# Two moves in a four-layer network kernel: the split of the last ffn's weights, and who mixes the second conditioning's weights

## The chip, the cores and the metric

The kernel runs on one core of a Trainium2 chip. The metric is the device time of one execution in microseconds, as a median over runs. The engines are named as in the profile: PE (TensorE matmuls, PEld their weight loads), DVE (VectorE), ACT (ScalarE), POOL (GpSimd) and SP (SyncE, which issues the transfers).

## The reference, cut to what matters

The input x is 16 blocks of 128 tokens with 128 features, float32. Four layers each add an attention of a conditioned x and an ffn of a conditioned x. Two places matter here.

The second conditioning of layer 0 mixes eight weight matrices for each block, with eight factors, under one mask. The attention of layer 3 has 16 heads of width 8, is causal, and stands just ahead of the last conditioning and the last ffn:

```python
# layer 0, second conditioning: y is the (16, 8) cond_8, weight (8, O, T), mask (O, T)
W[b] = sum_g y[b, g] * weight[g] * mask          # one 128x128 matrix for each block b
x2[b] = x[b] @ W[b].T + bias

# layer 3
score = einsum('bnqd,bnkd->bnqk', Q, K) / sqrt(8), masked causally; attn = softmax(score)
out = einsum('bnqk,bnkd->bnqd', attn, V) @ W_o.T
# last ffn, on a conditioned x
h = silu((x @ w1.T) * s1) * ((x @ w2.T) * s2)
h = gelu((h @ h1.T) * sh1); h = gelu((h @ h2.T) * sh2); return (h @ w3.T) * s3
```

## The kernel before, in words

x stays on the chip for the whole kernel. The 16 blocks are worked on in four chunks of four blocks. One ordered list of steps (`order`) is built first. Each engine's program then walks the whole list and issues its own part of each step, with semaphore waits between engines. So the order of steps is the order of every engine's queue, and there is no planner.

Much of the list is written by `in_order`. It takes items that have several stages, starts one new item per round, and in each round emits the new item's first stage and then the next stage of every item that is still live, youngest first. An attention is a list of 32 such items called heads (chunk n, block or head group j, half 0 or 1), plus projection items. In the last attention (`mh_attn(3, ...)`) the stages of one head are, in five or six successive rounds:

- scores on PE (lines 1677 to 1693; the mask is added by line 1686, the products by line 1693), and for every second head the masked copy of the keys, `kb`, on POOL (line 2796);
- row maxima on DVE (line 2318, two of them), a subtraction on DVE (line 2321), then the exponentials on ACT (lines 2024 and 2028);
- transposes on PE (`turn4`, lines 1607 and 1608) and their eviction by ACT (line 2033);
- the product with V on PE (line 1734), and for the second half the division on DVE (lines 2327 and 2329);
- for the last head of a chunk the output projection on PE (line 1741) and its addition on DVE (line 2332).

Halves 0 are "early": they read only 64 keys per block, so their row maxima, exponentials and transposes are half as large. A head takes two of four PSUM banks (`RA`) for its scores. The first bank is given back by the subtraction on DVE, the second by the exponentials on ACT that read it. The transposes use two other banks (`RB`), and the projections of the next chunk (lines 1659 to 1667) use banks of both rings.

**The split of the last ffn's weights.** The last ffn multiplies float32 numbers as two float32r parts each: a rounded part and the rest. `split_steps` makes eleven steps `wsplit`, one for each 512 of 5632 columns. In a step ACT copies 512 columns of BW to R1 in the rounded type (line 2173), and DVE subtracts the rounded part from the original (line 2743), waiting for ACT. Step number s is put behind the first stage of item 6 + 2s of the last attention's item list, so items 6, 8, ... 26 carry one each. In ACT's queue it stands ahead of that round's exponentials, in DVE's queue ahead of that round's row maxima. The result is first read by the last ffn (`l3_up`), after the attention and a conditioning.

**The mixed weights of the second conditioning.** During the first attention, `wbot_steps` puts one step `wbot` beside each of the 32 heads: four blocks b to b+3 at a time, eight factors g. In a step DVE does block b alone (line 2341 for g = 0, otherwise the multiply-add at line 2344, which the profile books under its helper, line 2211), and POOL does blocks b+1 to b+3: a product of 384 columns into a small buffer (line 2806) and an addition of it (line 2810). The buffers (`RWB`) are two, of 384 columns. POOL's queue holds these steps between the `kb` copies that the scores need. The step `cond2` on PE (line 1755), whose first one comes while the last heads of the attention are finishing, waits for the last `wbot` of DVE and of POOL.

Of the kernel before, what the change touches and what calls it, by code (L numbers as in the profile page):

```python
# [6 lines left out]
ALU = mybir.AluOpType  # L7
# [136 lines left out]
def build(nc, xT, cst, l0b, w8, b2, fw, fd, l1c, moe1, l1f, moe2, moe3, l2f, moe4, l3f, xs, ys, out):  # L144
    with ExitStack() as ctx:
# [448 lines left out]
        WBOT = A1[:, 8192:10240].rearrange("p (b o) -> p b o", b=16)  # L594
        RWB = Ring([A1[:, 10240 + 384 * k:10624 + 384 * k] for k in range(2)])
        WUG = BW[:, 6144:6912].rearrange("p (n o) -> p n o", o=128)
        WDN = BW[:, 6912:7296].rearrange("p (n o) -> p n o", o=128)

        def wbot_steps():
            def masked():  # L600
                sig["wmask"] = tick("wmask")
                step("wmask")
            steps = [masked]
            for b in range(0, NB, 4):
                for g in range(8):
                    def go(b=b, g=g):
                        at = step("wbot", b=b, g=g, mask=sig["wmask"], prev=sig.get(("wb", b)), prev_pool=sig.get(("wb3", b)),
                                  tmp=RWB.take() if g else None)
                        at["t"] = sig["wb", b] = sig["wbot"] = tick("wbot_dve")
                        at["part"] = sig["wb3", b] = sig["wbot_pool"] = tick("wbot_pool")  # L610
                        if g:
                            at["acc"] = sig["wb3", b] = sig["wbot_pool"] = tick("wbot_pool")
                            RWB.give(at["tmp"], at["acc"])
                    steps.append(go)
            return steps
# [36 lines left out]
        for n in range(NC):  # L652
            def c2(n=n):
                at = step("cond2", n=n, x=sig["x0", n], wbot=sig["wbot"], wbot_pool=sig["wbot_pool"], pa=RA.take(),
                          yfree=sig["Yfree", n])
                at["mm"] = sig["wbot_over"] = tick("c2_mm")
                at["y"] = sig["y0b", n] = tick("c2_y")
                RA.give(at["pa"], at["y"])
            items.append(([("x0", n)], [c2], ("y0b", n)))
# [777 lines left out]
        def split_steps():  # L1437
            steps = []
            for k in range(0, LO, 512):
                def go(k=k):  # L1440
                    at = step("wsplit", k=k, over=sig["moe4_over"])
                    at["hi"] = tick("l3_act")
                    at["t"] = sig["l3w"] = tick("l3_vec")
                steps.append(go)
            return steps
# [108 lines left out]
        for k in range(6, 6 + 2 * len(splits), 2):  # L1554
            f0, go = at3[k][1][0], splits[(k - 6) // 2]
            at3[k] = (at3[k][0], [lambda f0=f0, go=go: (f0(), go())] + at3[k][1][1:], at3[k][2])
        seq = (items + flat(seq[12:]) + flat(mix(m3, f2, m4, shared_items())) + at3 + cond_items("y3b", 3, "x3")
# [39 lines left out]
        def _(e):  # L1597
# [27 lines left out]
            for kind, at in order:  # L1625
# [122 lines left out]
                elif kind == "cond2":  # L1748
                    over(at["pa"])
                    w.wait_ge(*at["wbot"])  # L1750
                    w.wait_ge(*at["wbot_pool"])
                    w.wait_ge(*at["x"])
# [231 lines left out]
        def _(e):  # L1984
# [7 lines left out]
            for kind, at in order:  # L1992
# [171 lines left out]
                elif kind == "s2_up":  # L2164
                    for k in range(2):
                        over(at["r"][k])
                        w.wait_ge(*at["mm"][2 * k])
                        e.activation(at["r"][k].ap, at["pg"][k].ap, ACT.Silu).then_inc(at["silu"][k][0], 1)
                elif kind == "wsplit":
                    k = at["k"]  # L2170
# [28 lines left out]
        def _(e):  # L2199
# [17 lines left out]
            for kind, at in order:  # L2217
# [115 lines left out]
                elif kind == "wmask":  # L2333
                    w.wait_ge(*loaded["w8"])
                    e.tensor_tensor(W8, W8, bc_mid(c("maskT"), 8), ALU.mult).then_inc(sig["wmask"][0], 1)
                elif kind == "wbot":
                    b, g = at["b"], at["g"]
                    y = COND[:, 8 * b + g:8 * b + g + 1]
                    w.wait_ge(*at["mask"])
                    if g == 0:  # L2340
                        e.tensor_scalar(WBOT[:, b, :], W8[:, g, :], y, None, ALU.mult).then_inc(at["t"][0], 1)
                    else:
                        w.wait_ge(*at["prev"])
                        stt(WBOT[:, b, :], W8[:, g, :], y, WBOT[:, b, :], ALU.mult, ALU.add).then_inc(at["t"][0], 1)
                elif kind == "fq":
# [391 lines left out]
                elif kind == "s2_down":  # L2737
                    w.wait_ge(*at["mm"])
                    e.tensor_tensor(ch(X, at["n"]), v4(at["pb"].ap), ch(X, at["n"]), ALU.add).then_inc(at["t"][0], 1)
                elif kind == "wsplit":  # L2740
                    k = at["k"]
# [29 lines left out]
        def _(e):  # L2771
# [6 lines left out]
            for kind, at in order:  # L2778
# [19 lines left out]
                elif kind == "wbot":  # L2798
                    b, g = at["b"], at["g"]
                    to = WBOT[:, b + 1:b + 4, :]  # L2800
                    yb = COND.rearrange("p (b g) -> p b g", g=8)[:, b + 1:b + 4, g]
                    part = at["tmp"].ap.rearrange("p (b o) -> p b o", b=3) if g else to
                    w.wait_ge(*at["mask"])
                    if g:
                        over(at["tmp"])
                    e.tensor_tensor(part, bc_mid(W8[:, g, :], 3), bc_last(yb, 128), ALU.mult).then_inc(at["part"][0], 1)
                    if g:
                        w.wait_ge(*at["part"])
                        w.wait_ge(*at["prev_pool"])
                        e.tensor_tensor(to, to, part, ALU.add).then_inc(at["acc"][0], 1)  # L2810
# [148 lines left out]
```

## Time and profile before

| | |
|---|---|
| time, median of 3 runs | 1377.66 us (1374.42 to 1378.32) |
| the profiled execution's own time | 1366.43 us |
| its span | 1364.6 us |
| PE busy | 1223.0 us (90%) |
| DVE busy | 841.5 us (62%) |
| ACT busy | 655.3 us (48%) |
| POOL busy | 270.6 us (20%) |
| first attention, by its scores | about 25 to 160 us |
| last attention, by its steps | about 1090 to 1230 us |

Busy time is an average over stages with different limits. What a change in one stage is worth has to be read in that stage, from the idle gaps of the engine that sets its pace and from what ended them. In the rows of a timeline the figures are start and length in microseconds, and in brackets the idle time of that engine just before, with what ended it.

### The profile page before, as it was taken

Reading aid. Unit: us, or ns where it says so; the run is one execution under the profiler, and the core shown is the slowest. Engines: PE = TensorE matmul, PEld = TensorE weight load, DVE = VectorE, ACT = ScalarE, POOL = GpSimd, SP = SyncE. Lnnn points to the kernel's source line nnn. Section 1 sums busy time; section 2 is a strip of 40 time slices with the busy share of each in tenths; the row PEclk is TensorE's granted clock in tenths of the full one; section 3 lists DMA queues with packets and bytes.
Section 4 is the critical chain, followed back from the end, with each engine's and each line's share of the span. In section 5 each row is a group of like instructions: output and inputs, shape, how many; then the busy total and the mean of one; then the engine's idle time right before and its main releaser. Section 6 shows DMA issues by size and latency. Waiting matters only on the chain.

```text
span 1364.6 us, 27739 instructions
## 1 busy us (share of the span) xinstructions
PE 1223.0 (90%) x10063; PEld 961.5 (70%) x10063; DVE 841.5 (62%) x1813; ACT 655.3 (48%) x1338; POOL 270.6 (20%) x381
## 2 busy tenths in 40 slices
PE   5999880889999899999999999899999998888999
PEld 2555530458788889887887888489888855556777
DVE  4989769664556576657777565566564466764242
ACT  2665677445433334444454444234434365655553
POOL 5756200120003143330000013044230121100000
PEclk9999995999999999999999999999999999999999
DMA  9000020401042113104106101032120000000000
GB/s 323 2 1 2 2 77 0 197 12 63 9 200 80 59 55 98 51 27 159 50 6 255 54 7 49 24 113 69 34 83 16 1 2 2 3 2 1 0 16 16
DMA packets 42898, 75.86 MB, mean 56 GB/s; under 512 B 3848, under 2 KB 33680, under 8 KB 41872
## 3 DMA queue, kind: packets, MB, share of 16 engines
q1 hardware_dynamic: 38672, 65.69, 13.3%
q0 software_dynamic: 4096, 8.40, 2.1%
q8 instruction: 86, 1.41, 0.5%
q14 instruction: 44, 0.36, 0.1%
HBM read 59.78 MB, written 14.29 MB: 54 GB/s over the span
## 4 chain that ended last, share of the span: by engine, by line
PE 71%; DVE 16%; ACT 7%; issue 4%; DVEq 1%; DMA 1%; POOL 0%; ACTq 0%; SPq 0%; POOLq 0%
PE bank L1866 7%; PE bank L1877 7%; PE bank L1862 7%; PE bank L1921 5%; PE bank L1853 4%; PE bank L1931 3%; PE bank L1607 3%; PE bank L1612 3%; PE bank L1614 3%; PE bank L1613 3%; PE bank L1846 2%; PE bank L1848 2%; PE bank L1847 2%; DVE SM L2318 2%; PE bank L1677 2%
## 5 line engine op out<-in xcount | busy, mean ns | idle before, releaser
L2124 ACT ACTIVATE SC<-bank 128x512 f32<-128x512 f32 x192 | 114.4, 596 | 224.2 <-PE bank L1862 126.7
L2211 DVE SCALAR_TENSOR_TENSOR SC<-bank,SM,SC 128x512 f32<-128x512 f32 x128 | 95.8, 748 | 123.4 <-PE bank L1866 100.4
L1877 PE MATMUL bank<-A,SC 128*128 x1024 | 137.0, 277 | 7.9 <-DVE SC L2211 7.1
L1866 PE MATMUL bank<-X,SC 128*128 128x128 f32 x1024 | 137.5, 278 | 4.0 <-DVE SC L2495 3.5
L1862 PEld LDWEIGHTS bank<-X,SC 128*128 128x128 f32 x1024 | 126.8, 193 | 20.0 <-issue 13.0
L1862 PE MATMUL bank<-X,SC 128*128 128x128 f32 x1024 | 136.9, 277 | 3.7 <-ACT SC L2108 2.5
L1877 PEld LDWEIGHTS bank<-A,SC 128*128 128x128 f32 x1024 | 125.4, 192 | 17.3 <-issue 16.5
L1866 PEld LDWEIGHTS bank<-X,SC 128*128 128x128 f32 x1024 | 125.4, 193 | 6.3 <-DVE SC L2495 6.1
L1921 PE MATMUL bank<-A 128*128 128x128 f32 x736 | 100.0, 279 | 11.5 <-DVE A L2645 8.7
L1921 PEld LDWEIGHTS bank<-A 128*128 128x128 f32 x736 | 89.8, 192 | 15.9 <-ACT A L2149 8.9
L2796 POOL TENSOR_SCALAR A<-A,CC 128x256 f32<-128x256 f32 (+1 forms) x128 | 56.3, 459 | 215.3 <-DVE A L2303 106.3
L2024 ACT ACTIVATE A<-bank,SM 128x128 f32<-128x128 f32 (+1 forms) x256 | 70.2, 367 | 59.7 <-DVE SM L2318 59.6
L2108 ACT ACTIVATE SC<-A 128x512 f32 x128 | 80.6, 629 | 28.5 <-PE bank L1866 22.8
L2846 POOL DMA_INDIRECT A<-ys,POSI x64 | 62.6, 978 | 130.7 <-PE bank L1915 39.2
L2834 POOL DMA_INDIRECT xs<-CC,POSI x64 | 63.3, 989 | 117.0 <-DVE POSI L2624 28.3
L2475 DVE TENSOR_TENSOR SC<-bank,SC 128x512 f32<-128x512 f32 x64 | 44.3, 692 | 64.3 <-PE bank L1848 52.8
L2318 DVE TENSOR_REDUCE SM<-bank 128x4 f32<-128x512 f32 (+1 forms) x128 | 73.3, 613 | 7.1 <-PE bank L1677 4.8
L1931 PE MATMUL bank<-BW,A 128*128 x552 | 77.4, 277 | 0.0
L1612 PE MATMUL bank<-R 128*128 128x512 f32 x176 | 69.4, 394 | 7.6 <-DVE SC L2211 6.1
L1931 PEld LDWEIGHTS bank<-BW,A 128*128 128x128 f32 x552 | 70.2, 194 | 1.9 <-issue 1.7
L2821 POOL TENSOR_TENSOR SM<-SM 128x32 f32<-128x32 f32 x32 | 8.3, 259 | 315.5 <-DVE SM L2211 313.6
L1613 PE MATMUL bank<-R 128*128 128x512 f32 x176 | 68.6, 390 | 0.0
(342 smaller groups left out, 2528.9 us busy)
## 6 DMA issues: line engine op xcount, KB each, us to landing
A<-in_moe SPq DMA_DIRECT2D x36, 768.0 KB, 10.1
A<-xs SPq DMA_DIRECT2D x20, 256.0 KB, 3.9
ys<-A SPq DMA_DIRECT2D x20, 256.0 KB, 2.3
BW<-in_l1f SPq DMA_DIRECT2D x2, 2048.0 KB, 7.7
BW<-in_l2f SPq DMA_DIRECT2D x1, 3456.0 KB, 12.1
BW<-in_l1c SPq DMA_DIRECT2D x1, 3072.0 KB, 17.0
BW<-in_l3f SPq DMA_DIRECT2D x1, 2816.0 KB, 10.0
A<-in_l1c SPq DMA_DIRECT2D x1, 2560.0 KB, 8.4
```

The costliest lines, as they stand in the source:

```text
L1612: e.matmul(o, wh, hi, start=start, stop=False)
L1613: e.matmul(o, wh, lo, start=False, stop=False)
L1862: m = e.matmul(at["pg"].ap[:, cut(q)], wx[:, cut(q)], x, start=True, stop=True)
L1866: m = e.matmul(at["pu"].ap[:, cut(q)], wx[:, cut(4 + q)], x, start=True, stop=True)
L1877: m = e.matmul(o, at["h"].ap[:, cut(q)], W[:, bass.ds(r + (1024 + 128 * q), 128)], start=k == 0 and q == 0, stop=k == 1 and q == 3)
L1921: m = e.matmul(at["pa"].ap[:, cut(q)], at["wt"].ap[:, cut(q)], at["x"].ap, start=True, stop=True)
L1931: m = e.matmul(o, at["ht"].ap[:, cut(q)], BW[:, bass.ds(r + (dn + 128 * q), 128)], start=q == 0, stop=q == nk - 1)
L2024: a = e.activation(s[:, k * (4 + r):k * (5 + r)], at["pa"][1].ap[:, k * r:k * r + k], ACT.Exp, bias=at["m"].ap[:, 4 + r:5 + r])
L2108: e.activation(at["wx"].ap[0][:, 0:512], MOE_AT[at["L"]][:, bass.ds(r, 512)], ACT.Identity).then_inc(at["g"][0], 1)
L2124: e.activation(at["h"].ap, at["pg"].ap, ACT.Gelu_apprx_tanh).then_inc(at["gelu"][0], 1)
L2211: return e.scalar_tensor_tensor(out=o, in0=a, scalar=s, in1=b, op0=o1, op1=o2)
L2318: e.tensor_reduce(m[:, 4 * x:4 * x + 4], pa[x], AX, ALU.max, negate=True).then_inc(at["max"][x][0], 1)
```

## The change

The split is cut in two steps. `wround` holds ACT's rounding and stays at items 6, 8, ... 26. `wrest` holds DVE's subtraction and goes behind the first stage of the item that follows, 7, 9, ... 27. The mixed weights are now made by POOL alone, four blocks in one instruction of 512 columns, with two buffers of 512 columns; DVE's part of the step and PE's wait for it are gone.

```diff
-        RWB = Ring([A1[:, 10240 + 384 * k:10624 + 384 * k] for k in range(2)])
+        RWB = Ring([A1[:, 10240 + 512 * k:10752 + 512 * k] for k in range(2)])
...
                     def go(b=b, g=g):
-                        at = step("wbot", b=b, g=g, mask=sig["wmask"], prev=sig.get(("wb", b)), prev_pool=sig.get(("wb3", b)),
-                                  tmp=RWB.take() if g else None)
-                        at["t"] = sig["wb", b] = sig["wbot"] = tick("wbot_dve")
-                        at["part"] = sig["wb3", b] = sig["wbot_pool"] = tick("wbot_pool")
+                        at = step("wbot", b=b, g=g, mask=sig["wmask"], prev=sig.get(("wb", b)), tmp=RWB.take() if g else None)
+                        at["part"] = sig["wb", b] = sig["wbot"] = tick("wbot_pool")
                         if g:
-                            at["acc"] = sig["wb3", b] = sig["wbot_pool"] = tick("wbot_pool")
+                            at["acc"] = sig["wb", b] = sig["wbot"] = tick("wbot_pool")
                             RWB.give(at["tmp"], at["acc"])
...
             for k in range(0, LO, 512):
-                def go(k=k):
-                    at = step("wsplit", k=k, over=sig["moe4_over"])
-                    at["hi"] = tick("l3_act")
+                u = {}
+
+                def rounded(k=k, u=u):
+                    at = step("wround", k=k, over=sig["moe4_over"])
+                    at["hi"] = u["hi"] = tick("l3_act")
+
+                def rest(k=k, u=u):
+                    at = step("wrest", k=k, hi=u["hi"])
                     at["t"] = sig["l3w"] = tick("l3_vec")
-                steps.append(go)
+                steps.append((rounded, rest))
...
         for k in range(6, 6 + 2 * len(splits), 2):
-            f0, go = at3[k][1][0], splits[(k - 6) // 2]
-            at3[k] = (at3[k][0], [lambda f0=f0, go=go: (f0(), go())] + at3[k][1][1:], at3[k][2])
+            for at, go in zip((k, k + 1), splits[(k - 6) // 2]):
+                f0 = at3[at][1][0]
+                at3[at] = (at3[at][0], [lambda f0=f0, go=go: (f0(), go())] + at3[at][1][1:], at3[at][2])
...
@@ PE, cond2
                     w.wait_ge(*at["wbot"])
-                    w.wait_ge(*at["wbot_pool"])
...
@@ DVE
-                elif kind == "wbot":
-                    b, g = at["b"], at["g"]
-                    y = COND[:, 8 * b + g:8 * b + g + 1]
-                    w.wait_ge(*at["mask"])
-                    if g == 0:
-                        e.tensor_scalar(WBOT[:, b, :], W8[:, g, :], y, None, ALU.mult).then_inc(at["t"][0], 1)
-                    else:
-                        w.wait_ge(*at["prev"])
-                        stt(WBOT[:, b, :], W8[:, g, :], y, WBOT[:, b, :], ALU.mult, ALU.add).then_inc(at["t"][0], 1)
...
@@ POOL, wbot
-                    to = WBOT[:, b + 1:b + 4, :]
-                    yb = COND.rearrange("p (b g) -> p b g", g=8)[:, b + 1:b + 4, g]
-                    part = at["tmp"].ap.rearrange("p (b o) -> p b o", b=3) if g else to
+                    to = WBOT[:, b:b + 4, :]
+                    yb = COND.rearrange("p (b g) -> p b g", g=8)[:, b:b + 4, g]
+                    part = v4(at["tmp"].ap) if g else to
...
-                    e.tensor_tensor(part, bc_mid(W8[:, g, :], 3), bc_last(yb, 128), ALU.mult).then_inc(at["part"][0], 1)
+                    e.tensor_tensor(part, bc_mid(W8[:, g, :], 4), bc_last(yb, 128), ALU.mult).then_inc(at["part"][0], 1)
                     if g:
                         w.wait_ge(*at["part"])
-                        w.wait_ge(*at["prev_pool"])
+                        w.wait_ge(*at["prev"])
                         e.tensor_tensor(to, to, part, ALU.add).then_inc(at["acc"][0], 1)
```

## Rows read from the trace of the kernel before

**Rows 1.** Who waited for whom, 1105 to 1184 us: total, times, longest.

```profile
DVE R L2743 <- ACT R L2173: 20.1, 10, 2.9
```

**Rows 2.** Busy time of each engine in three stretches of the last attention.

```profile
1105.00:1184.00 79.00, 66.56 (x1349) 42.32 (x1341) 52.04 (x97) 47.28 (x139) 13.58 (x36) 1.00 0.01 2
1112.36:1119.09 6.73, 5.75 (x139) 3.79 (x136) 4.64 (x10) 4.77 (x14) 1.41 (x4) 1.00 0.01 2
1195.40:1200.91 5.51, 5.51 (x141) 3.71 (x143) 4.22 (x9) 4.25 (x15) 0.00 (x0) 1.00 0.01 3
```

**Rows 3.** Timeline, two rounds of the last attention with a split, to the next split.

```profile
1111.07 0.65 ACT L2173 ACTIVATE R<-BW 128x512 fp32r<-128x512 f32 x1
1111.76 0.69 DVE L2743 TENSOR_TENSOR R<-BW,R 128x512 fp32r<-128x512 f32 x1 [2.06 <-ACT R L2173]
...
1113.68 1.14 ACT L2024 ACTIVATE A<-bank,SM 128x128 f32<-128x128 f32 x4 [1.96 <-DVE SM L2318]
...
1117.80 0.65 ACT L2173 ACTIVATE R<-BW 128x512 fp32r<-128x512 f32 x1
```

**Rows 4.** Timeline, later rounds without a split.

```profile
1196.13 0.76 DVE L2318 TENSOR_REDUCE SM<-bank 128x4 f32<-128x256 f32 x2 [0.61 <-PE bank L1693]
...
1199.14 1.29 DVE L2318 TENSOR_REDUCE SM<-bank 128x4 f32<-128x512 f32 x2 [0.18 <-PE bank L1693]
...
1199.60 1.09 ACT L2033 ACTIVATE A<-bank 128x512 f32<-128x512 f32 x2 [1.26 <-PE bank L1608]
```

**Rows 5.** Timeline of PE around the projections and after the last split.

```profile
1135.35 1.16 PE L1663 MATMUL bank<-CC,Y 128*128 128x128 f32 x8 [0.46 <-DVE A L2303]
1137.28 1.09 PE L1667 MATMUL bank<-CC,Y 128*64 128x128 f32 x8 [0.77 <-DVE A L2303]
1142.40 1.12 PE L1741 MATMUL bank<-A,CC 128*128 128x512 f32 x2 [2.42 <-DVE A L2321]
...
1168.48 1.10 PE L1659 MATMUL bank<-Y,CC 128*128 128x512 f32 x2 [1.83 <-ACT SC L2033]
...
1186.06 0.28 PE L1686 MATMUL bank<-MKB,IDB 128*128 128x256 bf16 x1 [1.45 <-DVE A L2321]
```

**Rows 6.** Groups of DVE instructions by shape, 30 to 160 us: busy, mean ns, idle before.

```profile
L2211 DVE SCALAR_TENSOR_TENSOR A<-A,CC 128x128 f32<-128x128 f32 x28 | 14.5, 517 | 0.0
...
L2341 DVE TENSOR_SCALAR A<-A,CC 128x128 f32<-128x128 f32 x4 | 2.7, 665 | 0.0
```

**Rows 7.** Timeline of PE, three gaps in the first attention.

```profile
55.17 1.98 PE L1677 MATMUL bank<-A 64*128 64x512 f32 x4 [2.08 <-ACT A L2024]
...
91.74 1.13 PE L1677 MATMUL bank<-A 64*128 64x512 f32 x4 [0.74 <-ACT A L2024]
...
145.39 1.13 PE L1677 MATMUL bank<-A 64*128 64x512 f32 x4 [2.95 <-DVE A L2321]
```

**Rows 8.** Timeline of DVE with POOL idle (44 us), and with POOL busy (139 us).

```profile
44.13 0.34 DVE L2211 SCALAR_TENSOR_TENSOR A<-A,CC 128x128 f32<-128x128 f32 x1
44.39 0.17 DVE L2208 TENSOR_SCALAR SM<-SM 128x24 f32<-128x24 f32 x1
...
138.92 1.18 DVE L2211 SCALAR_TENSOR_TENSOR A<-A,CC 128x128 f32<-128x128 f32 x1
...
140.02 0.80 DVE L2269 TENSOR_SCALAR SM<-SM 128x16 f32<-128x16 f32 x1
```

**Rows 9.** The chain of work in order of time: start, length, what.

```profile
50.87 0.91 DVE A L2211
```

**Rows 10.** Timeline: start and end of POOL's last burst, first product of cond2.

```profile
118.49 1.84 POOL L2796 TENSOR_SCALAR A<-A,CC 128x256 f32<-128x256 f32 x4 [12.12 <-DVE A L2211]
...
144.64 0.99 POOL L2810 TENSOR_TENSOR A<-A 128x384 f32<-128x384 f32 x1
...
159.77 1.16 PE L1755 MATMUL bank<-X,A 128*128 128x128 f32 x8
```

**Rows 11.** POOL's group of 256 columns, whole span: busy, mean ns, idle before.

```profile
L2815 POOL TENSOR_TENSOR A<-A 128x256 f32<-128x256 f32 x16 | 12.9, 804 | 49.6 <-DVE A L2430 49.6
```

More of the change, by code:

```diff
@@ L653, in c2 @@
             def c2(n=n):
-                at = step("cond2", n=n, x=sig["x0", n], wbot=sig["wbot"], wbot_pool=sig["wbot_pool"], pa=RA.take(),
+                at = step("cond2", n=n, x=sig["x0", n], wbot=sig["wbot"], pa=RA.take(),
                           yfree=sig["Yfree", n])
@@ L2168, in _ @@
                         e.activation(at["r"][k].ap, at["pg"][k].ap, ACT.Silu).then_inc(at["silu"][k][0], 1)
-                elif kind == "wsplit":
+                elif kind == "wround":
                     k = at["k"]
@@ L2739, in _ @@
                     e.tensor_tensor(ch(X, at["n"]), v4(at["pb"].ap), ch(X, at["n"]), ALU.add).then_inc(at["t"][0], 1)
-                elif kind == "wsplit":
+                elif kind == "wrest":
                     k = at["k"]
```

## Prediction, made before the changed kernel was run

> **What bounds the kernel now.** I read the page first: PE is busy for nine tenths of the span, so an edit on another engine is worth only the PE gaps that it closes. The change touches two attentions, so I then asked who waited for whom there. In the last attention DVE's subtraction of the split waited 20.1 us for ACT's rounding, ten times of its eleven [rows 1]. That is more than a side wait if DVE is what PE waits for, so I took the busy times by stretch. From 1105 to 1184 us, where the eleven splits stand, PE is busy 66.56 of 79.00 us: 12.44 us idle. Two rounds with a split take 6.73 us with PE busy 5.75; two rounds without one, a little later, take 5.51 us with PE busy all the time [rows 2].
>
> The timeline shows why. ACT starts the rounding at 1111.07, behind its evictions of the round before. DVE, idle for 2.06 us, subtracts at 1111.76 and only then takes the row maxima, which need nothing of the split. ACT, idle for 1.96 us, gets the maxima at 1113.68, works through exponentials and evictions without a gap, and reaches the next rounding at 1117.80 [rows 3]. This is a closed loop: 0.69 us (rounding) + 0.60 (subtraction, start to start of what follows) + 1.32 (maxima, to the start of ACT) + 4.12 (ACT to its next rounding) = 6.73 us. PE, with 5.5 us of work, runs behind it. The reader is to see that DVE waits for ACT and ACT for DVE within one round, in turn.
>
> In the first attention the chain of work passes mostly through PE, but from about 121 to 145 us through DVE. DVE spends 14.5 + 2.7 us on 32 small multiply-adds of the mixed weights [rows 6]. One takes 0.34 us while POOL is idle and up to 1.18 us while POOL works [rows 8].
>
> **Part 1, the split in two rounds.** No instruction is added or removed: eleven copies on ACT, eleven subtractions on DVE. What goes is DVE's wait, since the rounding is a round old when the subtraction comes. The loop is cut: rounding and maxima now run side by side.
>
> Is there room, so that PE becomes the bound? Take the two rounds without a split and put both pieces in. ACT has 1.26 us idle there and gets 0.65. DVE has 0.61 us idle before the early maxima and 0.18 before the late ones [rows 4] and gets 0.60 to 0.69. Up to item 12 the rounding falls before the late exponentials and the subtraction before the early maxima: it fills the 0.61 us gap, and delays nothing by more than 0.1 us. From item 16 on the parity is the other: the subtraction stands before the late maxima, which slip 0.4 us, and ACT has to make up 0.3 of that and 0.65 of rounding out of its 1.26. That fits too, and the banks that the next scores need come free 0.5 us or more before PE asks. So I put these rounds at PE's pace of 5.51 us. DVE's work with a split, 4.64 us, and ACT's 4.77 [rows 2] lie below it.
>
> The sum starts from PE's idle time in the stretch, 12.44 us. The waits for the rotated keys and queries at two projections stay: 0.46 + 0.77 us at the first, the same at the second, together 2.46 [rows 5]. The wait for the output projection at 1142.40, 2.42 us, goes: DVE is free for the maxima 3.3 us earlier. The wait of the second projection at 1168.48, 1.83 us, is for evictions behind early exponentials that waited behind the subtraction; ACT still has to round, so I leave 0.55 of it. The subtraction of that split now lands behind the projection's DVE work, where ACT is busy for as long: nothing. The wait of 1.45 us at 1186.06 lies outside the stretch and goes. In the four regular pairs the period falls by 1.22 us while PE's idle time is 0.98 [rows 2], as its weight loads run closer together: 4 x 0.24 = 1.0 more. Sum: 12.44 - 2.46 - 0.55 + 1.45 + 1.0 = 11.9 us gained. The ends: if only the subtraction's own 0.6 us leaves the loop, 11 x 0.6 = 6.6 us; if no projection wait is left, about 13.
>
> **Part 2, POOL alone.** DVE loses 32 instructions, 17.2 us busy [rows 6]. Most lie beside PE's work. I count those that lead to a PE gap in the timeline. Around 48 to 52 us two of them (0.82 and 0.91 us of the chain [rows 9]) lead to the gap of 2.08 us at 55.17: 1.7 us. At 88 us one (0.68) leads to the gap of 0.74 at 91.74: 0.7 us. From 121 to 145 us six lie on the chain, 3.5 us together, the last of them 1.18 long [rows 8], before PE's gap of 2.95 us at 145.39 [rows 7]. Sum 5.9 us.
>
> Against it stand longer POOL instructions. Three small DVE operations at 140 to 142.7 us took 0.80, 0.76 and 0.76 us where such a one takes 0.17 beside an idle POOL [rows 8], and each ended as a POOL instruction ended. With POOL instructions a third longer they wait about 0.8 us longer in all. The SBUF page of the Trainium skill (SBUF — State Buffer, Who interferes with whom) gives the rule: a port pair shared by the two engines is locked for a whole instruction, and a DVE instruction with two SBUF inputs or in a two-port mode blocks behind a GpSimd one that reads SBUF. It speaks against this change, since 512 columns hold the lock a third longer, and for it, since 32 victims go. By it the three cost 0.8 us more; without it nothing would be subtracted. The trace agrees with it, by 0.80 us against 0.17.
>
> So part 2 gives 5.9 - 0.8 = 5.1 us if POOL is hidden. No row has a 512-column POOL instruction. I go by what POOL did: its last burst runs from 118.49 to 145.63 us, with four kb copies (4 x 1.84 = 7.4 us) and 21 instructions of 384 in the other 19.8, 0.94 each. Times 4/3: 26.4 + 7.4 = 33.8 us, to 152.3. The first product of cond2 came at 159.77 [rows 10] and comes 2.7 us sooner relative to the burst (3.5 - 0.8): 157.1. Hidden by 4.8 us. The kb copies between slip by 1.3 us per pair of heads and were 9 us or more early in this burst. The lower end is 0.94 us, if columns cost nothing more; the upper is the row of 256 columns, 804 ns [rows 11], or 3.14 ns a column: 1.61 us each, 33.8 + 7.4 = 41.2, to 159.7, and PE would wait 2.6 us. I take 4/3, since 384 is nearest in size, and the same two operations. The earlier bursts end in idle times of 7 us and more (12.12 us before the last [rows 10]) and only fill these. The wait of PE that goes was long over: nothing.
>
> **Sum.** 11.9 + 5.1 = 17.0 us. The profiled execution took 1366.43 us (span 1364.6 and 1.8 around it), so it would take 1349.4. The median of the runs is 11.2 us above it. I carry that over: 1377.66 - 17.0 = 1360.7, say 1361 us.
>
> **Rivals.**
> - *The split is cut, but only the subtraction leaves the loop.* The rounding still stands before the exponentials, and the new place of the subtraction may hold the late maxima. For it: the DVE gap there is only 0.18 us [rows 4]. Against: ACT has 1.26 us. Part 1 gives 6.6 us: 1377.7 - 6.6 - 5.1 = 1366 us.
> - *POOL is late for cond2 or slows DVE's rest.* With the row of 256 columns PE waits 2.6 us, and with part 2's gaps taken up by other waits it gives nothing: 1377.7 - 11.9 = 1366 us. For it: DVE had slack in most rounds. Against: the chain from 121 to 145 us.
> - *PE's slow spell goes as well.* After the gap at 55.17 the matmuls took 1.98 us for 1.13 [rows 7], and so until 59 us, some 1.9 us lost. With a shorter gap it may not happen: 1359 us. It may as well turn up elsewhere.
> - *Slower: POOL becomes the bound of the first attention.* If its instructions grow far more than their columns, cond2 waits for the burst. To eat 17 us it must end at 157.1 + 17 = 174.1 us, so (174.1 - 118.5 - 7.4) / 21 = 2.3 us each, against 0.94 now; at 2.6 us the kernel takes 1384 us. For it: nothing but the unseen shape; against: the upper bound of 1.61.
>
> **How the numbers follow.** Chances: 0.66 for the forecast (with the spell, 1356 to 1364), 0.13 for the first rival, 0.12 for the second, 0.06 for the spell case alone, 0.03 for the slower one. The range takes in the first two rivals (1366) above and, below, 13 us for part 1 with the spell gone (1358), and on either side 3 to 5 us for the spread of medians (the runs shown lie 4 us apart): 1353 to 1369. A difference under 0.3% (4.1 us) can't be told from no change here. Faster by more: 0.94; within: 0.03; slower: 0.03.
>
> **What would show it.** Right: no wait of line 2743 for ACT, pairs of rounds with a split near 5.5 us, the stretch of the splits near 67 to 68 us; the gap at 145.39 mostly gone, POOL instructions of 512 columns near 1.1 to 1.3 us, the last of them some 5 us before cond2. Wrong: PE gaps before line 1686 released by ACT's exponentials in rounds 16 to 22; PE's first L1755 released by POOL; small DVE operations well over 1 us.

## The result, and the profile after

The changed kernel took 1352.5 us (median of 4 runs, 1351.77 to 1353.68) against 1377.63 us (4 runs): a ratio of 0.9834, 95% interval [0.9818, 0.9851], so 20.5 to 25.1 us faster. The forecast was 1361 us, 17.0 us faster, in a range of 1353 to 1369: the time came out at its lower end (the median 0.5 us below it, the ratio times the time before, 1354.8 us, just inside). Both parts went the way that was said, and both gave more than was counted in sum, though not at every place.

The two profiled executions lie closer together: 1366.43 us before and 1353.68 us after, 12.7 us apart. That is a warning about single executions and it comes back below.

From the page of the changed kernel, the busy time by engine:

```profile
PE 1222.1 (90%) x10063; PEld 960.2 (71%) x10063; DVE 830.8 (61%) x1781; ACT 653.7 (48%) x1338; POOL 285.1 (21%) x381
```

DVE lost 10.7 us of busy time and POOL gained 14.5, and neither figure is the gain: PE does what it did. The 32 instructions taken from DVE had been busy for 17.2 us [rows 6], so the rest of its work shows 6.5 us more; one row of that comes below. The gain is in the stages.

**The last attention.** Who waited for whom in the changed kernel, 1090 to 1172 us (total, times, longest), against 20.1 us in [rows 1]:

```profile
DVE R L2737 <- ACT R L2176: 0.8, 4, 0.2
```

Busy times of two rounds with a split, of the stretch of the splits, and of five rounds in it (the answers to [rows 2]; columns are length, then busy time with count of PE, weight loads, DVE, ACT and POOL, the granted clock as a share of full speed, DMA share, GB/s):

```profile
1109.77:1115.28 5.51, 5.51 (x140) 3.71 (x138) 4.83 (x10) 4.76 (x15) 1.41 (x4) 1.00 0.02 6
1104.30:1173.40 69.10, 66.55 (x1360) 42.59 (x1364) 53.74 (x99) 49.37 (x147) 13.81 (x36) 1.00 0.01 3
1138.67:1153.39 14.72, 14.68 (x362) 9.62 (x364) 13.81 (x28) 13.39 (x41) 5.04 (x12) 1.00 0.01 2
```

The pair of rounds takes 5.51 us where it took 6.73, with PE busy all the time. In the third row DVE is busy 13.81 of 14.72 us, so by estimate one more DVE operation of 0.9 us in these rounds would make DVE the next bound. The timelines of ACT and DVE for one split, beside [rows 3], and every PE gap of the changed kernel from 1090 to 1180 us, beside [rows 5]:

```profile
1109.77 0.63 ACT L2176 ACTIVATE R<-BW 128x512 fp32r<-128x512 f32 x1
```

```profile
1110.44 0.69 DVE L2737 TENSOR_TENSOR R<-BW,R 128x512 fp32r<-128x512 f32 x1 [0.21 <-ACT R L2176]
```

```profile
1130.40 1.16 PE L1667 MATMUL bank<-CC,Y 128*128 128x128 f32 x8 [0.46 <-DVE A L2306]
1132.32 1.09 PE L1671 MATMUL bank<-CC,Y 128*64 128x128 f32 x8 [0.77 <-DVE A L2306]
1160.77 1.16 PE L1667 MATMUL bank<-CC,Y 128*128 128x128 f32 x8 [0.46 <-DVE A L2306]
1162.70 1.09 PE L1671 MATMUL bank<-CC,Y 128*64 128x128 f32 x8 [0.77 <-DVE A L2306]
```

The two gaps that were forecast to stay are there to the hundredth (0.46 and 0.77 at each projection), and those of 2.42, 1.83 and 1.45 us are gone.

**The first attention.** PE's gaps that answer to [rows 7], in the changed kernel:

```profile
54.65 1.13 PE L1681 MATMUL bank<-A 64*128 64x512 f32 x4 [1.61 <-ACT A L2027]
...
89.35 1.13 PE L1681 MATMUL bank<-A 64*128 64x512 f32 x4 [0.18 <-ACT A L2027]
...
138.82 1.13 PE L1681 MATMUL bank<-A 64*128 64x512 f32 x4
...
144.35 1.13 PE L1681 MATMUL bank<-A 64*128 64x512 f32 x4 [0.88 <-DVE X L2335]
...
153.19 1.16 PE L1758 MATMUL bank<-X,A 128*128 128x128 f32 x8
```

The gap at 55 us shrank from 2.08 to 1.61 us only; the matmuls behind it take 1.13 us where they took 1.98. The matmuls that waited 2.95 us at 145.39 now start at 138.82 with no gap. The gap of 0.88 us behind them is not new; the kernel before had it too:

```profile
150.93 1.13 PE L1677 MATMUL bank<-A 64*128 64x512 f32 x4 [0.88 <-DVE X L2332]
```

POOL by shape from 30 to 160 us (busy, mean ns), first the kernel before, then the changed one:

```profile
L2810 POOL TENSOR_TENSOR A<-A 128x384 f32<-128x384 f32 x28 | 29.3, 1046 | 2.2
L2806 POOL TENSOR_TENSOR A<-A,CC 128x384 f32<-128x384 f32 x31 | 26.0, 840 | 0.0
```

```profile
L2804 POOL TENSOR_TENSOR A<-A 128x512 f32<-128x512 f32 x28 | 36.6, 1307 | 2.2
L2800 POOL TENSOR_TENSOR A<-A,CC 128x512 f32<-128x512 f32 x31 | 33.6, 1085 | 0.0
```

A product and an addition together went from 1.886 to 2.392 us, a factor of 1.27 for 4/3 of the columns. The last burst of the changed kernel starts at 116.04 and ends at 147.9:

```profile
146.65 1.27 POOL L2804 TENSOR_TENSOR A<-A 128x512 f32<-128x512 f32 x1
```

The first product of cond2 comes at 153.19: POOL is done 5.3 us ahead of it (forecast 4.8).

**Where PE's time lies, step by step.** Both kernels issue the same 10063 PE instructions in the same order, so the start of the k-th in one trace can be set against the k-th in another, and each step of the difference is a gain at its place. The change against before: 6.8 us from 30 to 160 us, 13.6 us from 1100 to 1190 us, 20.4 together. In this one trace 7.7 us of it were given back, 6.5 of them between 260 and 960 us, in stages that the change doesn't touch. Is that a cost of the change or chance? That is what the first experiments ask, with the split of the gain over its two parts.

### The profile page after: what moved, and what is told of

It reads as the page before. It is cut to its first block, busy times and chain, and to the rows that moved or that the text cites. A ratio compares the mean times of both kernels' runs of the same rounds, so it can differ in the third digit from the quotient of the medians.

```text
span 1351.9 us, 27707 instructions
## 1 busy us (share of the span) xinstructions
PE 1222.1 (90%) x10063; PEld 960.2 (71%) x10063; DVE 830.8 (61%) x1781; ACT 653.7 (48%) x1338; POOL 285.1 (21%) x381
## 3 DMA queue, kind: packets, MB, share of 16 engines
q8 instruction: 86, 1.41, 0.4%
## 4 chain that ended last, share of the span: by engine, by line
PE 76%; DVE 13%; ACT 5%; issue 3%; DVEq 1%; DMA 1%; POOL 0%; ACTq 0%; SPq 0%; POOLq 0%
PE bank L1869 7%; PE bank L1880 7%; PE bank L1865 7%; PE bank L1924 5%; PE bank L1611 4%; PE bank L1856 4%; PE bank L1934 3%; PE bank L1616 3%; PE bank L1618 3%; PE bank L1617 3%; PE bank L1681 2%; PE bank L1849 2%; PE bank L1851 2%; PE bank L1850 2%; PE bank L1697 2%
## 5 line engine op out<-in xcount | busy, mean ns | idle before, releaser
L2828 POOL DMA_INDIRECT xs<-CC,POSI x64 | 63.7, 996 | 119.3 <-DVE POSI L2618 28.1
## 6 DMA issues: line engine op xcount, KB each, us to landing
BW<-in_l2f SPq DMA_DIRECT2D x1, 3456.0 KB, 10.7
BW<-in_l1c SPq DMA_DIRECT2D x1, 3072.0 KB, 16.7
```

## Experiments

Each kernel was timed beside the kernel before on the same chip. Four chips were used, and on them the kernel before took 1370.51 us (the next four kernels), 1368.85 (the four after them), 1373.55 (the first two with filled gaps) and 1370.28 (the last two), medians of 9 to 17 runs. So ratios carry across chips, not times.

### The kernel before again, each part alone, the change again

The edits: nothing; only the hunks of the split; only the hunks of the mixed weights; the change as it is.

> The kernel before, unchanged, timed against itself. Both theories: ratio 1.000. It is run for its spread and its second trace. Theory A (the gain lies in the two attentions alone, and what differs elsewhere is chance): its trace differs from the first one between 260 and 1100 us by some us, with single slow spells of PE at other places, as much as the changed kernel's did (6.5 us). Theory B (the change moves the middle stages too): the two traces of the kernel before agree there within 1 us.

> The kernel before with the split in two rounds, and the mixed weights as before. Theory A: the stretch of the last attention shrinks as in the changed kernel, by 13.6 us from the first rounding to 1220 us; time 0.990 of before (13.6 of 1377). Theory B (the two parts need each other or the middle stages carry part of the gain): clearly more or less than this, with the difference outside the last attention.

> The kernel before with the mixed weights by GpSimd alone, and the split as before. Theory A: the first attention is 6.6 us shorter up to the first product of cond2, nothing in the last; time 0.995 of before. Theory B: the 6.6 us are given back by 1100 us, as in the trace of the changed kernel, because an earlier start meets the transfers of the middle stages: time 1.000.

> The changed kernel once more, for a second trace and a closer ratio. Theory A: PE's distance to the kernel before is -6.6 us at the end of the first attention, within 3 us of that up to 1100 us in this trace (the 6.5 us lost there in the first one were chance), and 13.6 us more at the end: ratio 0.985. Theory B: the 6.5 us are lost again at the same places (265, 500 and 890 to 940 us), ratio 0.990.

| kernel | us | ratio [95%] | PE steps, first attention | PE steps, last attention |
|---|---|---|---|---|
| before again | 1371.22 | 1.0005 [0.9986, 1.0025] | +1.5 | +1.5 |
| split alone | 1354.62 | 0.9878 [0.9856, 0.9900] | +2.9 | -13.6 |
| POOL alone | 1361.28 | 0.9932 [0.9912, 0.9952] | -6.8 | +1.6 |
| both | 1344.65 | 0.9816 [0.9795, 0.9838] | -6.8 | -13.6 |

The steps are us by which PE is later (+) or earlier (-) than in the first trace of the kernel before, from 30 to 160 us and from 1080 to 1200 us. By the steps the parts are independent, and by their ratios they add up: 16.7 + 9.3 = 26.0 us against 25.2 for both. The last attention's 13.6 us is the same in every trace with the split. The 6.5 us that the first trace of the change lost in the middle are not in its second: there PE is 9.2 us ahead at 1080 us. So they were chance, and no cost of the change.

The timings gave more than was expected of them (0.990, 0.995 and 0.985). Each part gains 2.5 to 3.1 us more in its ratio than on its steps. For POOL alone that lies inside the interval (6.6 to 12.1 us for steps of 6.8), for the split just outside (13.7 to 19.7 for 13.6), and for both together it is clear (22.2 to 28.1 for 20.4). The traces show one thing that comes and goes between runs of one kernel: short stretches in which PE is granted 1.2 instead of 2.4 GHz, each costing 1.3 to 1.7 us where PE is busy. Those in the two attentions stand behind PE's longer gaps. The gap at 55 us in the second trace of the kernel before and with the split alone:

```profile
56.08 1.13 PE L1677 MATMUL bank<-A 64*128 64x512 f32 x4 [2.06 <-ACT A L2024]
```

```profile
55.64 1.36 PE L1683 MATMUL bank<-A 64*128 64x512 f32 x4 [2.07 <-ACT A L2030]
```

And the granted clock (the share behind POOL's busy time) behind the gaps at 55, 145 and 1142 us: the kernel before, the same again, the split alone, POOL alone.

```profile
55.30:58.70 3.40, 3.40 (x12) 1.84 (x12) 3.40 (x7) 2.02 (x7) 3.40 (x5) 0.50 0.00 0
145.40:148.80 3.40, 3.40 (x60) 2.40 (x60) 2.52 (x6) 2.79 (x8) 0.23 (x1) 1.00 0.02 5
1142.40:1145.80 3.40, 3.40 (x52) 2.05 (x52) 1.85 (x3) 2.37 (x7) 0.00 (x0) 1.00 0.00 0
```

```profile
57.45:60.85 3.40, 3.26 (x12) 1.62 (x10) 3.40 (x7) 2.93 (x9) 3.40 (x7) 0.51 0.00 0
146.15:149.55 3.40, 3.17 (x10) 1.69 (x11) 2.77 (x6) 2.79 (x9) 0.48 (x1) 0.50 0.02 5
1146.25:1149.65 3.40, 3.30 (x12) 1.11 (x12) 1.24 (x3) 1.62 (x5) 0.00 (x0) 0.50 0.00 0
```

```profile
56.45:59.85 3.40, 3.40 (x14) 2.07 (x12) 3.40 (x7) 2.46 (x7) 3.40 (x6) 0.50 0.00 0
145.30:152.00 6.70, 6.18 (x56) 4.22 (x60) 3.06 (x6) 4.55 (x12) 0.76 (x1) 0.50 0.01 2
```

```profile
55.31:58.71 3.40, 3.15 (x16) 1.49 (x16) 3.40 (x7) 2.62 (x8) 3.32 (x5) 1.00 0.01 2
1136.15:1139.55 3.40, 3.40 (x14) 1.02 (x14) 1.61 (x3) 1.28 (x4) 0.00 (x0) 0.51 0.00 0
```

A share of 0.50 is 1.2 GHz. Note that the same gap is followed by the low clock in one execution of the kernel before and not in the other (145 and 1142 us), and that the gap at 55, with 2.06 to 2.08 us of idle, was followed by it in all three traces of the old mixing in which nothing filled it. With the new mixing and 512 columns the gap is 1.61 us, and in none of the eight traces does the clock fall there.

### What made the split dear: its round or its place in DVE's queue?

The subtraction stays in the rounding's round, but behind that round's row maxima:

```diff
-            for at, go in zip((k, k + 1), splits[(k - 6) // 2]):
-                f0 = at3[at][1][0]
-                at3[at] = (at3[at][0], [lambda f0=f0, go=go: (f0(), go())] + at3[at][1][1:], at3[at][2])
+            rounded, rest = splits[(k - 6) // 2]
+            ...                                    # rounded: behind stage 0 of item k, as before
+            at, s = (k - 1, 1) if len(at3[k - 1][1]) > 1 else (k - 2, 2)
+            ...                                    # rest: behind stage s of item at
```

> The changed kernel, but each subtraction of the split back in the round of its rounding, behind that round's row maxima instead of ahead of them. Theory A (what cost the time was that DVE waited for ACT in front of the maxima; the round is indifferent): the last attention is as short as in the changed kernel within 1 us, 13.6 us less than before. Theory B (the subtraction needs to be a round away, else DVE still waits): the rounding is done before the maxima end, so a wait would show in DVE's queue at line 2743's successor, and the stretch is 5 us or more longer than in the changed kernel.

It took 1345.75 us, 0.9827 [0.9797, 0.9857], and its steps in the last attention are 13.6 us again. Who waited for whom on DVE, 1090 to 1175 us:

```profile
DVE R L2740 <- ACT R L2179: 4.2, 8, 1.1
```

DVE still waits 4.2 us in eight waits, up to 1.1 us, and PE's gaps are the same four (0.46 and 0.76 to 0.77 us). So these waits cost nothing, and the round is not what matters. What cost 13.6 us was that the row maxima, for which ACT waited, stood behind the waiting instruction. Both places tested that come behind these maxima give the whole gain.

### How much room does POOL have?

POOL issues each product twice, which makes its step about 1.1 us longer:

```diff
+                    e.tensor_tensor(part, bc_mid(W8[:, g, :], 4), bc_last(yb, 128), ALU.mult).then_inc(at["pre"][0], 1)
+                    w.wait_ge(*at["pre"])
                     e.tensor_tensor(part, bc_mid(W8[:, g, :], 4), bc_last(yb, 128), ALU.mult).then_inc(at["part"][0], 1)
```

> The changed kernel with the product of 512 columns issued twice in each mixing step on GpSimd (same output). A step grows from 2.35 to about 3.5 us. GpSimd's last burst, 116.0 to 147.9 us, grows by 11 x 1.14 = 12.5 us to 160.4, and the first product of cond2, at 153.2 in the changed kernel, must wait for it. Theory A (GpSimd had 5.3 us of slack there and is hidden elsewhere): PE waits 7 us once, ahead of cond2, perhaps a slow spell of 1.7 us with it; nothing else: 7 to 9 us slower than the changed kernel. Theory B (the kb copies between the steps have no slack, GpSimd binds the whole attention): PE gaps ahead of the scores released by GpSimd, 15 us or more slower.

It took 1357.11 us, 0.9922 [0.9895, 0.9949], 11.4 us above the kernel of the section before and 12.8 us above that of the next, all on the same chip: more than the 7 to 9 us of the one theory and less than the 15 of the other. PE's waits in its first attention, and the clock behind the last one:

```profile
45.50 1.13 PE L1682 MATMUL bank<-A 64*128 64x512 f32 x4 [1.42 <-DVE A L2325]
...
142.74 1.13 PE L1682 MATMUL bank<-A 64*128 64x512 f32 x4 [1.32 <-DVE A L2325]
...
163.04 2.04 PE L1759 MATMUL bank<-X,A 128*128 128x128 f32 x8 [5.85 <-POOL A L2807]
```

```profile
161.00:167.70 6.70, 4.66 (x36) 4.30 (x40) 0.00 (x0) 2.58 (x7) 1.81 (x2) 0.50 0.00 0
```

PE waits 5.85 us for POOL's last addition, which ends at 162.9: the bound has changed as the slower rival had it. Against the change's trace PE is 12.0 us later at 170 us: 6.15 at cond2, 2.0 behind it at the low clock, and 3.9 ahead of 150 us (4.4 at four places, less 0.4 that this trace was ahead before the first). The expectation had only the place at cond2. At the four places PE waits for DVE, not for POOL. DVE is late there because a small operation on it took over 1 us beside POOL. The ones ahead of PE's gaps at 45.50 and 142.74 us (those ahead of the gaps of 0.75 us at 81.98 and 1.25 at 117.08 took 1.24 us each):

```profile
41.80 1.23 DVE L2287 TENSOR_TENSOR A<-Y 128x4 f32<-128x4 f32 x1
...
139.13 1.14 DVE L2215 SCALAR_TENSOR_TENSOR SM<-SM 128x32 f32<-128x32 f32 x1
```

The first of them in the changed kernel, where POOL is idle at that moment:

```profile
42.20 0.16 DVE L2286 TENSOR_TENSOR A<-Y 128x4 f32<-128x4 f32 x1
```

So the 5.3 us of slack at cond2 is real, but more work on POOL is paid for elsewhere too, through what it does to DVE: 0.8 to 1.4 us at each place where a slowed operation stands ahead of the row maxima and the subtraction that PE's next scores wait for.

### What do longer POOL instructions cost DVE?

POOL mixes three of the four blocks, so its instructions have 384 columns as before and DVE still does none; the mixed weights of every fourth block are left out, and cond2 uses its neighbour's for it:

```diff
-                    to = WBOT[:, b:b + 4, :]
+                    to = WBOT[:, b + 1:b + 4, :]
...
-                        m = e.matmul(at["pa"].ap[:, cut(j)], WBOT[:, b, :], X[:, b, :], start=True, stop=True)
+                        m = e.matmul(at["pa"].ap[:, cut(j)], WBOT[:, max(b, 4 * at["n"] + 1), :], X[:, b, :], start=True, stop=True)
```

> The changed kernel, with GpSimd mixing three of four blocks as before and nobody the first (its product takes the next block's matrix; the output lacks that mix). It has DVE's relief without the longer GpSimd instructions. Theory A (the longer instructions block DVE's two-input and small operations longer and ate 1.2 us of the gap at 55 us): the first attention is 1 to 1.5 us shorter than in the changed kernel, at 50 to 60 us. Theory B (the forecast overrated that gap; the gap's end is set by PE or ACT): equal within 0.3 us.

1344.32 us, 0.9815 [0.9785, 0.9844]; its first attention gains 6.84 us where the change gains 6.78. In sum the longer instructions on POOL cost nothing, but place by place they do. DVE's addition of 768 columns ahead of the gap at 55 us takes 0.95 us here and 1.54 in the changed kernel, and the gap is 1.02 us here and 1.61 there:

```profile
51.06 0.95 DVE L2350 TENSOR_TENSOR A<-A,SM 128x768 f32<-128x768 f32 x1
...
54.53 1.13 PE L1681 MATMUL bank<-A 64*128 64x512 f32 x4 [1.02 <-ACT A L2027]
...
55.98 1.38 DVE L2354 TENSOR_SCALAR A<-A 128x768 f32<-128x768 f32 x1
...
60.79 0.55 PE L1611 MATMUL bank<-CC,A 128*128 128x128 f32 x3 [0.45 <-ACT A L2036]
```

Here another DVE operation meets POOL instead (1.38 us; 0.55 in the second trace of the change), and PE gives back 0.5 us at 60.79, where the changed kernel has no gap. So theory A was right of the gap, with 0.6 us for its 1.2, and theory B of the sum: what these collisions cost goes by which DVE operation falls beside which POOL instruction, not by length alone. The other rows of the changed kernel show the same: the addition is slowed, and of the small operations that had taken 0.80, 0.76 and 0.76 us the first two now take 0.16 and 0.20:

```profile
50.59 1.54 DVE L2350 TENSOR_TENSOR A<-A,SM 128x768 f32<-128x768 f32 x1
...
134.73 0.16 DVE L2272 TENSOR_SCALAR SM<-SM 128x16 f32<-128x16 f32 x1
...
135.22 0.20 DVE L2276 TENSOR_TENSOR SM<-SM 128x16 f32<-128x16 f32 x1
```

POOL was at its `kb` copies then, four short ones in a row:

```profile
134.29 1.85 POOL L2790 TENSOR_SCALAR A<-A,CC 128x256 f32<-128x256 f32 x4
```

In the kernel with three blocks POOL is at a product and an addition instead, and the last two of the small operations take 0.59 and 0.76 us.

### The rest of DVE's queue between 120 and 145 us

On the changed kernel, the steps that compute the routing are put up to 12 heads earlier, so that DVE is freer ahead of 145 us:

```diff
-        for k, f in enumerate(fs + rt):
+        for k, f in enumerate(fs):
...
+        for k, f in enumerate(rt):
+            beside_heads[11 + 2 * k].append(f)
```

> The changed kernel with the five routing steps of DVE (maxima, indices, weights) taken from beside heads 23 to 27, where DVE sets the pace (PE gap of 1.13 us at 124 us), to beside heads 11 to 19, where PE is busy throughout. Theory A (DVE's work there sets PE's pace): 1 to 3 us less between 120 and 145 us, nothing more before: ratio to the kernel before 0.980 against 0.982. Theory B (DVE has no room at the new place either): the same time moves to 65 to 110 us, no gain.

1346.67 us, 0.9837 [0.9809, 0.9865]. From 120 to 150 us it gains 4.2 us on the kernel before, as the change does, so the move brings nothing there; from 85 to 100 us it falls 1.4 us behind the change, with a new gap of PE of 0.76 us at 93.69, which DVE ends.

### Are the low-clock stretches bound to the gaps?

The kernel has a step `keep_on(n)`, n products with the identity that nobody reads, to keep PE busy. In the kernel before, such fillers go into the three gaps of 2.08, 2.95 and 2.42 us; in the changed one, into those of 1.41 and 0.88 us ahead of the stretch at 165 us.

```diff
+                            if i == 0 and (n, j, half) in ((0, 3, 1), (3, 2, 0)):
+                                keep_on(3 if n == 0 else 4)
...
+                                if i == 3 and n == 0:
+                                    keep_on(3)
```

```diff
+                                if i == 0 and n == NC - 1:
+                                    keep_on(2)
...
+                if n == NC - 1:
+                    keep_on(1)
```

> The kernel before, with PE kept at work in its three longest gaps of the two attentions by products of the identity that nobody reads: 3 (1.4 us) ahead of the scores at 55 us (gap 2.08), 4 (1.9 us) ahead of those at 145 (gap 2.95), 3 ahead of the output projection at 1142 (gap 2.42). They fit in the gaps, so without slow spells the time is that of before. Theory A (the slow spells of PE that the kernel before shows behind these gaps, at 55 to 58 us in three traces of three, at 146 and at 1146 in two of three, follow from the gaps, and their loss is the part of the gain that the paths don't hold): no spell at these places, 3 to 5 us faster than before in the mean, ratio 0.997, and the scatter of the runs smaller. Theory B (spells come whatever PE does): ratio 1.000, spells at the same places.

> The changed kernel with PE kept at work in the two gaps at 163 to 165 us, by 2 products of the identity ahead of the last output projection of the first attention and 1 ahead of the last product of cond2 (1.4 us in 1.41 + 0.88 of gap). Theory A (spells follow gaps): the spell at 165 us, which every trace of the new mixing but one shows, goes, and 1 to 1.7 us with it: ratio to the kernel before 0.981 against 0.982. Theory B: no change.

The first took 1381.97 us, 1.0055 [1.0042, 1.0069]: slower. I had mis-sized the fillers. One product takes 0.95 us, so three overfill a gap of 2.08, and the filler at 145 us itself waited for its bank:

```profile
146.16 6.62 PE L1774 MATMUL bank<-CC 128*128 128x512 f32 x8 [3.90 <-ACT A L2037]
```

As a timing it says nothing of the theory. Its trace does: no low clock behind the gaps at 55 and 1142 us that were filled, and a long one behind the one at 145 that had become longer. The second took 1349.05 us, 0.9822 [0.9808, 0.9836]: the low clock at 165 us is gone, and no time was gained by it.

So once more with two products each in two of the gaps, leaving 145 us as it was, and the change beside it:

```diff
+                            if i == 0 and (n, j, half) == (0, 3, 1):
+                                keep_on(2)
...
+                                if i == 3 and n == 0:
+                                    keep_on(2)
```

> The kernel before with two of its gaps filled to size: one product of the identity takes 0.95 us (that of the fillers tried before), so 2 ahead of the scores at 55 us (1.9 us in 2.08) and 2 ahead of the output projection at 1142 (1.9 in 2.42). Theory A (slow spells follow gaps): none at 55 to 58 and none at 1142 to 1147; it saves 1.7 us at the first place always and at the second in two executions of three, 2.8 us in the mean: ratio 0.998. Theory B (spells come whatever PE does): a spell at 55 to 58 as in every trace with the old mixing and this gap, ratio 1.000.

> The changed kernel a third time, for a ratio on the same chip as the filled gaps. Theory A: 0.982, its runs within 3 us of each other, with no slow spell before 160 us but the one at 25. Theory B: 0.982 as well, with spells anywhere.

Timeline of PE and granted clock in the kernel with two gaps filled:

```profile
53.42 1.98 PE L1774 MATMUL bank<-CC 128*128 128x512 f32 x4
...
55.56 1.13 PE L1681 MATMUL bank<-A 64*128 64x512 f32 x4 [0.16 <-ACT A L2028]
...
145.25 2.08 PE L1681 MATMUL bank<-A 64*128 64x512 f32 x4 [2.93 <-DVE A L2325]
```

```profile
55.56:58.96 3.40, 2.56 (x14) 1.49 (x16) 3.40 (x8) 2.02 (x7) 3.40 (x4) 1.00 0.00 0
145.25:148.65 3.40, 3.40 (x12) 1.86 (x12) 2.53 (x6) 2.80 (x8) 0.24 (x1) 0.55 0.02 5
1143.00:1146.40 3.40, 2.90 (x27) 1.19 (x17) 2.49 (x4) 1.44 (x6) 0.00 (x0) 1.00 0.02 5
```

Full clock where the gap was filled, 55% of it behind the one left open. But its time is 1369.37 us, 0.9993 [0.9975, 1.0011]: the expected gain of about 0.2% can't be told from none, and its trace has two low stretches at 1172 and 1193 us that neither trace of the kernel before has. They too begin at gaps, which nothing had filled: those of 1.82 and 1.45 us behind which both traces of the kernel before kept the full clock. The change took 1345.29 us, 0.9826 [0.9807, 0.9844].

No version here beats the changed kernel: those nearest to it lie inside each other's intervals.

## Why the prediction was right, point by point

**The loop of ACT and DVE.** Right, and shown by the kernel with the subtraction behind the maxima: the loop was closed by the order in DVE's queue, and is cut by both orders tested in which the maxima don't stand behind the wait. ACT and DVE had the room that was read from their idle times; PE sets the pace at 5.51 us.

**Part 1, the sum** (11.9 forecast, 13.6 measured in every trace with the split), by PE's steps:

| term | forecast | measured |
|---|---|---|
| four regular pairs | 4.9 | 4.9 |
| output projection | 2.4 | 2.5 |
| left-over pairs, 1145 to 1166 us | 1.8 | 2.5 |
| second projection | 1.3 | 1.9 |
| last split | 1.45 | 1.8 |

Two terms were mis-sized. I left 0.55 us of the second projection's wait, because ACT still has to round there; nothing stayed. And I counted the weight loads that run closer together for the four regular pairs alone; each later release shows them as well: PE gains 0.06 to 0.17 us more there than the gap that went. Behind the last split a second gap, of 0.29 us, went as well but for 0.04. The gaps of a row are a lower bound for what goes with them.

**Part 2** (5.1 forecast, 6.8 measured). At 55 us 1.7 was forecast and the gap gave 0.5. The two multiply-adds went, each 0.83 us from its start to the next one's, but ahead of the division DVE now waits for PE's product with V:

```profile
49.39 0.96 DVE L2330 RECIPROCAL A<-bank 128x128 f32<-128x128 f32 x1 [0.49 <-PE bank L1718]
```

So from start to start DVE is 1.06 us faster up to its addition of 768 columns, and by that the gap shrank in the kernel with three blocks; with 512 columns the slower addition (1.54 us for 0.95) takes 0.6 of it back. I had counted neither the wait nor this. The slow spell behind the gap, which I had made a rival with 0.06, went as well and gave 1.3 more. So that this place came near its 1.7 us, with 1.8, is luck: two terms were missing against it and one for it. Ahead of it, at 45 us, 0.26 us came that nobody had forecast. At 91 us 0.56 for 0.7. From 121 to 150 us 4.2 for 2.7: more than the 3.5 us on the chain went, and the 0.8 us that I subtracted for small operations blocked by longer POOL instructions was not paid there. The rule of the Trainium skill (SBUF — State Buffer, Who interferes with whom) holds in what it says of single instructions, by 1.18 against 0.34 us before and by 1.54 us for the operation of 768 columns, which took 0.95 before; what was wrong is where I booked it. At 140 us nothing was paid, since the small operations now fall beside the short `kb` copies; at 55 us 0.6 us was, where I had booked nothing. Three blocks instead of four, 384 columns instead of 512, moved such collisions and left the sum the same within 0.1 us; doubling the product made four of them, at 0.8 to 1.4 us each.

**POOL** was hidden, by 5.3 us for 4.8, with 1.09 and 1.31 us an instruction in the forecast 1.1 to 1.3.

**From the trace to the median.** I carried over that the median lay 11.2 us above the profiled execution, unchanged. In the changed kernel it lies 1.2 us below it, so this step failed. Here the rest of the difference sits: the steps sum to 20.4 us, and the ratios of the change in its three timings (0.9816 to 0.9834) give 23 to 25. The first trace of the kernel before was a lucky one; its second is 5.5 us longer with the same program: it has five stretches at the low clock that the first lacks, and lacks one of the first. The change shortens the three gaps behind which the clock often fell. Over all traces it fell behind the gap of 2.08 us at 55 in 3 of 3, of 2.42 at 1142 in 2 of 3, of about 2.95 or more at 145 in 4 of 5, and behind none of 1.61. That ties the clock to the gaps by place. That these stretches are the 2.5 to 5 us between steps and ratios is only argued: the experiment that filled two gaps could not show it in the time. They would not be all of it either. By these counts, with 1.5 us for each stretch, the two that the first trace lacked come to some 2.2 us in the mean (an estimate); the rest stays open.

## What to carry to other kernels

In a queue that runs in order, ask of each wait who needs the instruction behind it; an operation that waits costs nothing if what others wait for stands ahead of it, and moving it by one place may be enough. Read the room for it from the idle time of each engine in the rounds without the operation, and the gain from the gaps of the engine that sets the pace, gap by gap, remembering that another release may end each of them. Before giving one engine longer or more work, look on its neighbour's chain for small operations that would fall beside it, since one of 0.16 us can become one of 1.2. Compare kernels by steps of instruction starts, place by place, before reading anything from the difference of two single executions.

## What had not been expected of the hardware

A PE gap of 2 to 3 us in an otherwise busy stage can cost more than itself: behind it PE ran at 1.2 GHz for a few us, and the matmuls of 1.13 us took 1.98 to 2.08. It is not certain in any one run (1142 us: at full clock in one execution of the kernel before, at half in the next), and it makes executions of one program differ by several us. Nor is the size a sharp line: in one trace it followed gaps of 1.82 and 1.45 us that two others passed at full clock. A gap of 1.61 us was not followed by it in any trace of the new mixing, while at 165 us it did follow two gaps of 1.41 and 0.88 us close together, in the changed kernel's traces:

```profile
163.15 1.12 PE L1745 MATMUL bank<-A,CC 128*128 128x512 f32 x2 [1.41 <-DVE A L2332]
165.15 2.05 PE L1758 MATMUL bank<-X,A 128*128 128x128 f32 x8 [0.88 <-DVE X L2335]
```

A float32 product or addition of POOL grew by 0.25 us for 128 columns more, 1.9 to 2.0 ns a column, less than in proportion: the estimate from the row of 256 columns ([rows 11], 3.14 ns a column) would have been 0.3 to 0.5 us too high an instruction.
